# A two-layer transformer kernel: the weights of 16 experts loaded into the queries' place, the first expert's rows alone, and early sums placed behind a normalisation

## What is computed

```
x1  = layernorm(x + attention(x))        # 16 heads of 128+64, latent keys and values of rank 64, causal
top 8 of 64 experts per token (softmax of x1 @ router.T)
moe[t] = sum over its 8 experts e of  w[t,e] * (silu(g) * u) @ down[e],  g, u = split(x1[t] @ gate_up[e])
x2  = layernorm(x1 + moe)                # gate_up: 64 x 256 x 192, down: 64 x 96 x 256
f, i, v, q = x2 @ w_f, ...;  state = tanh(f) * state + sigmoid(i) * silu(v)     # a scan over the tokens
x3  = layernorm(x2 + silu(q * state) @ w_ro + ((x2 @ w_up) * silu(x2 @ w_gate)) @ w_down)
out = layernorm(x3 + shared expert + the top 2 of 8 larger experts)
```

## Time and profile before

| | |
|---|---|
| median of 3 runs | 835.47 us (831.17 to 835.5) |
| the profiled execution's own time | 835.53 us |
| its span in the profile | 833.7 us |
| PE busy | 780.8 us, 94% |
| DVE, ACT, POOL busy | 565.5, 397.6, 272.0 us |
| attention, to its last score block | to 412 us of the span |
| 64 experts | 428 to 537 us |
| mixing | 547 to 621 us |

### The profile page before, as it was taken

How to read it: one execution, slowest core, us unless ns; L and a number is a source line. 1 busy time by engine, 2 the same in 40 slices (tenths; PEclk the granted TensorE clock), 3 DMA queues, 4 the chain that set the end, 5 groups by cost and what they waited for, 6 DMA issues and landing times.

```text
span 833.7 us, 16672 instructions
## 1 busy us (share of the span) xinstructions
PE 780.8 (94%) x4645; PEld 662.9 (80%) x4645; DVE 565.5 (68%) x1422; ACT 397.6 (48%) x898; POOL 272.0 (33%) x357
## 2 busy tenths in 40 slices
PE   7999989999999999999897999998889999999997
PEld 6888867778778777777697898897888778888786
DVE  5323778777877777777644677458857367777766
ACT  1325656655566666666323444312333256666531
POOL 2004445443343333230354565614422500000061
PEclk9998999999999999999998999999998999999999
DMA  7449961000000000000559999777720335555431
GB/s 210 105 104 370 405 238 41 28 28 28 28 21 28 21 18 24 14 28 15 167 157 342 355 357 360 260 254 251 304 102 20 107 112 151 153 151 151 120 94 65
DMA packets 63032, 120.63 MB, mean 145 GB/s; under 512 B 18304, under 2 KB 31616, under 8 KB 62848
## 3 DMA queue, kind: packets, MB, share of 16 engines
q1 hardware_dynamic: 51984, 95.41, 34.9%
q0 software_dynamic: 7680, 21.51, 7.2%
q10 hardware_dynamic: 3312, 3.02, 1.0%
HBM read 76.13 MB, written 43.78 MB: 144 GB/s over the span
## 4 chain that ended last, share of the span: by engine, by line
PE 69%; DVE 12%; issue 7%; ACT 4%; DMA 3%; POOL 3%; SPq 1%; DVEq 0%; ACTq 0%; POOLq 0%
PE scores L1578 9%; PE scores L1577 9%; PE scores L1576 9%; PE probsT_ps L1687 6%; PE scores L1797 5%; PE acc_ps L1987 5%; PE acc_ps L1714 4%; PE misc_ps L1702 4%; PE misc_ps L1700 3%; DVE xT_lo L1054 2%; PE misc_ps L1584 2%; DVE neg_max L1048 2%; PE scores L1807 2%; POOL xd_d L729 2%; PE scores L1840 2%
## 5 line engine op out<-in xcount | busy, mean ns | idle before, releaser
L778 ACT ACTIVATE area<-scores,neg_max 128x128 f32<-128x128 f32 (+7 forms) x128 | 94.9, 742 | 76.7 <-DVE neg_max L1048 75.7
L1048 DVE TENSOR_REDUCE neg_max<-scores 128x1 f32<-128x128 f32 (+7 forms) x128 | 95.7, 749 | 24.6 <-PE scores L1663 24.5
L1687 PE MATMUL probsT_ps<-ident,area 128*128 128x128 f32 x552 | 84.1, 277 | 12.9 <-DVE xT_lo L1054 12.0
L1054 DVE TENSOR_TENSOR xT_lo<-probsT_ps,xT_hi 128x512 fp32r<-128x512 f32 x92 | 62.9, 687 | 38.3 <-ACT xT_hi L785 36.7
L1687 PEld LDWEIGHTS probsT_ps<-ident,area 128*128 128x128 f32 x552 | 63.1, 143 | 24.9 <-issue 19.5
L658 POOL DMA_INDIRECT xe_d<-x_rows,send_i x64 | 64.1, 1001 | 55.8 <-ACT x_rows L802 38.8
L688 POOL DMA_INDIRECT ye_d<-area,home_i x64 | 61.4, 959 | 48.9 <-issue 23.0
L1797 PE MATMUL scores<-area 128*96 128x128 f32 x512 | 68.7, 278 | 1.1 <-DVE area L1220 0.6
L1576 PE MATMUL scores<-kT_hi,weff_hi 128*128 128x512 f32 (+3 forms) x172 | 67.1, 390 | 1.9 <-issue 1.3
L785 ACT ACTIVATE xT_hi<-probsT_ps 128x512 fp32r<-128x512 f32 x92 | 54.0, 594 | 25.1 <-PE probsT_ps L1687 24.8
L1797 PEld LDWEIGHTS scores<-area 128*96 128x96 f32 x512 | 60.5, 166 | 3.2 <-DVE area L1220 2.5
(11 more groups left out here) (258 smaller groups left out, 1944.5 us busy)
## 6 DMA issues: line engine op xcount, KB each, us to landing
area<-gate_up SPq DMA_DIRECT2D x32, 384.0 KB
area<-w SPq DMA_DIRECT2D x23, 512.0 KB, 3.9
xe_d<-area SPq DMA_DIRECT2D x8, 1088.0 KB, 11.3
area<-xe_d SPq DMA_DIRECT2D x32, 272.0 KB, 6.2
ye_d<-area SPq DMA_DIRECT2D x8, 1024.0 KB, 16.7
area<-ye_d SPq DMA_DIRECT2D x16, 512.0 KB, 4.9
area<-w SPq DMA_DIRECT2D x8, 1024.0 KB, 7.3
area<-down SPq DMA_DIRECT2D x32, 192.0 KB
```

The costliest lines, as they stand in the source:

```text
L778: act.activation(row_of(n)[:, 0:L], score_bank(n)[:, 0:L], ACT.Exp, bias=neg_max[:, n % 4:n % 4 + 1], accum_out=rsum[:, s, k:k + 1]).then_ ...
L1048: dve.tensor_reduce(neg_max[:, n % 4:n % 4 + 1], score_bank(n)[:, 0:(n // HEADS + 1) * P], AX.X, ALU.max, negate=True).then_inc(max_ready, 1)
L1054: dve.tensor_tensor(pT_lo[b % 3], seat_of("block", b)[:], pT_hi[b % 3].bitcast(f32), ALU.subtract).then_inc(lo_done, 1)
L1687: last = pe.transpose(seat_of("block", b)[:, i * P:(i + 1) * P], row_of(QUAD * G + i)[:, k * P:(k + 1) * P], ident[:])
```

## The change

The diff does seven things.

- `first_gu`, `first_dn`, `w_c` and `wo_c` are cut from `area1`, where the queries were. After the last split of queries (`q_split`) SP loads the weights of experts 0 to 15 there, in four pairs of transfers of 4 experts, and right behind them `w_c` and `wo_c`. `gate_up` and `down` read experts 0 to 15 from there.
- The ring of weights starts at expert 16. Its first 8 experts are loaded behind the rows of experts 8 to 14, with no wait of their own; from expert 24 on it is as before.
- The rows of expert 0 are loaded alone after send 0 has landed, those of expert 1 alone after send 1. Each has a semaphore.
- The rows of expert 8 and on follow the rows of expert 6 directly.
- The loops over experts on PE, DVE, ACT and POOL are written out as 64 experts. SP keeps a loop for experts 24 to 63.
- POOL's `sum_early(t + 2)` waits for `x2_done`, that is until DVE has normalised tile t+1.
- `w_c` now lies where experts 0 and 1 of `w1` go, so these two are loaded behind the last normalisation of mixing, and experts 2 to 7 during it.

```diff
+IN_ADVANCE = 16
-        w_c = cutC2(6, HC, HID)
-        wo_c = cutC2(2, HC, HID)
+        cutC1 = carve(area1)
+        w_c = cutC1(6, HC, HID)
+        wo_c = cutC1(2, HC, HID)
+        first_gu = cutC1(IN_ADVANCE * HC * 2 * I0).rearrange("p (e c n) -> p e c n", e=IN_ADVANCE, c=HC)
+        first_dn = cutC1(IN_ADVANCE, HID)[0:I0]
...
-        sent_last = moved[1::2]
+        sent_last = moved[0:2] + [moved[k | 1] for k in range(2, TOP0)]
...
-            sp.wait_ge(pT_ps, blocks_to(GROUPS))
-            for e in range(0, RING, 2):
-                load_weights(e, e)
-            sp.wait_ge(x1_done, TILES)
+            sp.wait_ge(q_split, TILES * PAIRS)
+            for e in range(0, IN_ADVANCE, 4):
+                sp.dma_start(first_gu[:, e:e + 4], gate_up0[:, e:e + 4]).then_inc(ld_first, 16)
+                sp.dma_start(first_dn[:, e:e + 4, :], down0[:, e:e + 4, :]).then_inc(ld_first, 16)
+            sp.dma_start(w_c, w_in).then_inc(ld_wc, 16)
+            sp.dma_start(wo_c, w_mix).then_inc(ld_wc, 16)
...
+            sp.wait_ge(pT_ps, blocks_to(GROUPS))
             for u in range(2):
                 sp.wait_ge(sent[u], 16 * (TILES - 1) * TOP0 // 2)
-            for e in range(0, RING, 2):
-                sp.wait_ge(sent_last[e // 2], 32)
+            for e in range(2):
+                sp.wait_ge(sent_last[e], 16)
+                sp.dma_start(xe[:, e:e + 1, :], xe_v[:, e:e + 1]).then_inc((ld_first_row, ld_xe[0])[e], 16)
+            for e in range(2, RING, 2):
+                sp.wait_ge(sent_last[e], 32)
                 load_rows(e, e)
-            sp.dma_start(w_c, w_in).then_inc(ld_wc, 16)
-            sp.dma_start(wo_c, w_mix).then_inc(ld_wc, 16)
-            with sp.Fori(1, E0 // RING) as i:
+            for e in range(RING, IN_ADVANCE + RING, 2):
+                load_rows(e, e % RING)
+                if e < 2 * RING:
+                    load_weights(IN_ADVANCE + e - RING, e % RING)
+            with sp.Fori(1 + IN_ADVANCE // RING, E0 // RING) as i:
...
-                load_w1(t)
+                if t + 2 < E1:
+                    load_w1(t + 2)
             sp.wait_ge(x3_done, TILES)
+            load_w1(0)
+            load_w1(1)
...
                 if before(t, TILES - 2):
+                    pool.wait_ge(x2_done, t + 2)
                     sum_early(t + 2, u)
...
-            for e in range(RING):
-                transpose_rows(e + 2, (e + 2) % RING)
-                gate_up(e + 1, (e + 1) % RING)
-                down(e, e)
-            with pe.Fori(1, E0 // RING - 1) as i:
...
-            for e in range(E0 - RING, E0):
+            for e in range(E0):
                 if e + 2 < E0:
                     transpose_rows(e + 2, (e + 2) % RING)
```

More of the change, by code:

```diff
@@ L309, in home_turn, with weights_of, await_weights @@
         def home_turn(e, u):
-            return turn(e, u) + (32 if u % 2 else 0)
+            return turn(e, u) + (16 if u < 2 else 32 if u % 2 else 0)
+        def weights_of(e):
+            if e < IN_ADVANCE:
+                return first_gu[:, e], first_dn[:, e, :]
+            return gu_w[:, e % RING], dn_w[:, e % RING, :]
+        def await_weights(eng, e):
+            if e < IN_ADVANCE:
+                eng.wait_ge(ld_first, 8 * IN_ADVANCE)
+            else:
+                eng.wait_ge(ld_gu[e % RING // 2], 2 * turn(e - IN_ADVANCE, e % RING))
         def steps_two(eng, body):
@@ L691, in _ @@
             pool.wait_ge(zeroed, 16 * ZEROINGS)
-            for e in range(RING):
[L693 to L696, removed]
+            for e in range(E0):
+                send_home(e, e % RING)
             def sum_early(t, u):
@@ L835, in _ @@
             expert_act(0, 0)
[L836 to L841, removed]
-                    expert_out(RING * i + u, u)
-            for e in range(E0 - RING, E0):
+            for e in range(E0):
                 if e + 1 < E0:
@@ L1228, in find_mine @@
             def find_mine(e, u):
+                if isinstance(e, int) and e == 0:
+                    dve.wait_ge(ld_first_row, 16)
                 dve.wait_ge(ld_xe[u // 2], turn(e, u))
@@ L1260, in _ @@
             gated(0, 0)
-            for e in range(RING):
-                copy_xeT(e + 2, (e + 2) % RING)
-                gated(e + 1, (e + 1) % RING)
-                if e % 2 == 0:
-                    find_mine(e + 2, (e + 2) % RING)
-                else:
-                    find_home(e + 1, (e + 1) % RING)
-            with dve.Fori(1, E0 // RING - 1) as i:
-                for u in range(RING):
-                    copy_xeT(RING * i + u + 2, (u + 2) % RING)
-                    gated(RING * i + u + 1, (u + 1) % RING)
-                    if u % 2 == 0:
-                        find_mine(RING * i + u + 2, (u + 2) % RING)
-                    else:
-                        find_home(RING * i + u + 1, (u + 1) % RING)
-            for e in range(E0 - RING, E0):
+            for e in range(E0):
                 if e + 2 < E0:
@@ L1780, in transpose_rows @@
             def transpose_rows(e, u):
-                pe.wait_ge(ld_xe[u // 2], turn(e, u))
+                if isinstance(e, int) and e == 0:
+                    pe.wait_ge(ld_first_row, 16)
+                else:
+                    pe.wait_ge(ld_xe[u // 2], turn(e, u))
                 if past(e, 2):
@@ L1791, in gate_up @@
                 pe.wait_ge(xeT_done, e + 1)
-                pe.wait_ge(ld_gu[u // 2], 2 * turn(e, u))
+                await_weights(pe, e)
                 if past(e, 2):
@@ L1797, in gate_up @@
                         last = pe.matmul(half[b][0:I0, part * P:(part + 1) * P],
[L1798 removed]
+                                         weights_of(e)[0][:, c, part * I0:(part + 1) * I0], xeT[:, b, c, :],
                                          start=c == 0, stop=c == HC - 1)
@@ L1806, in down @@
                     pe.wait_ge(ye_done, e - 1)
-                pe.matmul(half[2 + b][:, 0:HID], hT[:, b, :], dn_w[:, u, :], start=True, stop=True).then_inc(ye_ps, 1)
+                pe.matmul(half[2 + b][:, 0:HID], hT[:, b, :], weights_of(e)[1], start=True, stop=True).then_inc(ye_ps, 1)
             transpose_rows(0, 0)
```

13 lines of the change are left out of this document (4 added, 9 removed).

## The result

| | before | after |
|---|---|---|
| median of the runs (lowest to highest) | 834.96 us (831.17 to 835.5, 4 runs) | 824.05 us (820.88 to 828.25, 4 runs) |
| the profiled execution: time, span | 835.5, 833.7 us | 823.25, 821.2 us |
| first to last gate and up of the experts | 105.11 us | 97.85 us |
| first combine to last normalisation of mixing | 75.62 us | 72.22 us |

The ratio is 0.9887, with a 95% interval of 0.9845 to 0.993. The forecast was 823.2 us.

What follows compares the result with a forecast made beforehand. PE, busy 94% of the span, bounds the kernel, so gains come where it idles, runs at the lower clock or waits. Experts 8.2 plus mixing 4.1 make 12.3 off 835.5: 823.2 us, range 819.5 to 828.5.

Steps and rivals of the forecast that it cites:

- Part 1: Experts: 6.8 us of stall and lower clock plus 1.4 at the loops' edges come back, 8.2 in all.
- I take the full 8.2: Experts: the whole difference from undisturbed steps was taken as gain, bounds 6.5 and 9.1 us.
- the 1.4: Last 54 experts: 1.4 us lost at the loops' edges come back with written-out lists, unless transfers can't follow.
- Rival B: Later octets: transfers hold them at their old pace, experts gain 6.8, 824.6 us; chance 0.08, alone or with rival A.
- Part 2: First expert's rows loaded alone: no gain, since 40 identity matmuls cover their landing; bounds 0 and 0.
- Part 3: Mixing's early sums: five normalisations no longer run beside POOL's sum; 4.1 us gained, 2.0 if fully blocked.
- with 5 x 0.1: Mixing: a collision with POOL's sum costs a tenth of a microsecond in each of five tiles, leaving 4.1.
- rival A: Mixing: POOL's sum blocks the value product for its whole length, early sums gain only 2.0, 825.3 us; chance 0.13.
- Part 4: Later loads of w1 for experts 0 and 1, behind mixing's last normalisation: no gain, 25 us of cover.
- C: Experts: rows of expert 8 still come late, some 4 of the 6.8 stay, 827.2 us; chance 0.08.
- E: Mixing: POOL's last normalisation, now behind the sum, delays DVE's line 1332, giving back that gain, 827.3 us; chance 0.03.
- D: Experts: written-out lists starve as code comes through full transfer rings, 25 us lost, 848 us; chance 0.05.

Runs made afterwards that it cites:

- e3: The changed kernel with only the 2 MB of w_c and wo_c moved back behind the rows of experts 6 and 7: 829.29 us.
- e4: The changed kernel with experts 16 to 55 as loops of eight again on PE, DVE, ACT and POOL: 823.13 us.
- e1: The changed kernel without POOL's wait for x2_done before the early sum: 828.72 us.
- e5: The changed kernel with the rows of experts 0 and 1 loaded as a pair behind send 1 again: 866.52 us, where the kernel before took 869.08.
- e6: The changed kernel with ten groups of identity matmuls fewer ahead of the experts: 862.73 us, where the kernel before took 869.08.
- e2: The changed kernel with ACT's silu of the value left in PSUM, so DVE's value product has one SBUF input: 824.03 us.
- e13: The changed kernel again, unaltered, on another chip: 863.38 us (12 runs) against 867.31 before, ratio 0.9946.

## Why the prediction was right, and where it was off

The time is 0.85 us over the forecast by the medians and equal to it by the profiled execution (823.25). Both mechanisms are the ones predicted, and both terms were too large: together they gave 10.66 us instead of 12.3. That the profiled execution still met the forecast is luck. The missing 1.64 were made up by 1.84 in stretches where the sum had nothing: 0.88 ahead of the experts, 0.23 between them and mixing, 0.73 behind it.

**Part 1, 8.2 predicted, 7.26 measured.** The sum had 6.8 for the stall and 1.4 for the loops' edges. The three steps of the stall took 11.45 us and now take 4.58: 6.87 gained, and e3 shows the cause, since 5.8 of it return with the 2 MB alone. The 54 steps behind them gained 1.07 (84.77 to 83.70). The six steps ahead of them lost 0.68 (8.89 to 9.57), which "I take the full 8.2" left out: the rows of experts 4 and 5 came 0.54 late. The prediction looked only at experts 8 and 9. (Its 18 us for the transfers ahead were too few: the 2 MB landed at 391.8 and 394.0 instead of 388, at 313 GB/s instead of 362, which cost nothing 35 us ahead of the experts.) This lateness is not in every execution, it is in e4 (0.59) and not in e1 to e3. The weakest term is the 1.4. An edge does cost the 0.32 us that it takes in e4, but the written-out lists lose as much or more at the end: four steps 1.27 us too long in the changed kernel, and over all four written-out runs 83.70 to 84.98 for the 54 steps, where the kernel before has 84.77 and e4 84.03. The 1.07 is one draw from that spread. Rival B put this lag down to the transfers. For them speaks the wait for rows in the changed kernel, at a DMA share of 1.04; against them, that e1 and e3 wait for DVE's copy instead. What makes the end slow stays open.

**Part 2, nothing predicted, nothing measured.** The cover was the 40 groups of identity matmuls: the first transposes stand 8.9 us behind the first send before and after, in e5 with the pair too, and only fewer groups moved them (e6).

**Part 3, 4.1 predicted, 3.40 measured.** The step that was off is "with 5 x 0.1": the product pays 0.40, not 0.1. I had set the two scans of the last tile against rival A's mechanism, and the mechanism won: the product is held up until the sum ends, and e2 shows by what. The price I worked out for it, 0.5 in each tile, was nearly right. What A had wrong is the time: 5 x (0.93 - 0.40) = 2.65, and mixing gained 3.40. Tile by tile the steps fell by 0.27 in the first (8.73 to 8.46) and by 0.56, 0.62, 0.72, 0.62 and 0.62 in the next five. The first I had set at nothing, and it is nothing that can be told from chance: this step took anything from 8.00 (e4) to 9.21 (e13) in runs with the same code of mixing. In the five, 3.1 in all, 0.1 each is not accounted for.

The Trainium skill (SBUF — State Buffer, "Who interferes with whom") states that a DVE instruction with two SBUF inputs and a GpSimd instruction that reads SBUF contend, and that whichever comes first blocks the other for its whole length. The product and e2 agree with it (0.82 with two SBUF inputs, 0.42 with one). The 1.34 of the normalisation, which the prediction counts for it, are no case of two inputs: it has one of 128x256. The scans of the earlier trace rows, at most 0.58 instead of 0.484 inside POOL's normalisation, which has one large input, do not agree. Nor does a row just ahead of them that the prediction passed over, the product of the last tile itself. First before, then e2, where one of its inputs is in PSUM:

```profile
616.14 0.43 DVE L1314 SCALAR_TENSOR_TENSOR area<-area 128x256 f32<-128x256 f32 x1 [0.79 <-ACT area L865]
```

```profile
603.18 1.23 POOL L735 TENSOR_SCALAR x_rows<-y,mv,rstd 128x256 f32<-128x256 f32 x1
603.20 0.42 DVE L1323 SCALAR_TENSOR_TENSOR area<-area,probsT_ps 128x256 f32<-128x256 f32 x1 [0.78 <-ACT probsT_ps L887]
```

It began 0.04 behind POOL's normalisation and was not held up (0.43); POOL's took 1.48, and 1.23 in e2. So inside the one POOL instruction the product pays nothing and inside the other 0.40, and the prediction's row came from the wrong one. That POOL's sum reads two large inputs and its normalisation one may be why; no run shows it.

**Part 4, nothing.** ACT read its first `w1` at 641.25 instead of 654.49, without a wait: it moved with the rest.

**The rivals.** A came true in its mechanism and for three quarters of its price (0.40 of 0.53 in each tile). B's lag shows at the end of the stage alone, and its cause is not shown. C did not happen to expert 8; its like, late rows, did to expert 4, for 0.5 us. E did not happen: behind the sum the tiles stay regular. D did not happen on the first chip, where 57 of the changed kernel's 63 steps are undisturbed. On the others engines start late as D describes, whatever the cause, but in loops too, and the change is no slower than before.

## What to carry to other kernels

Where a stage begins with a wait for a transfer, ask what was issued in front of it: moving these 2 MB 60 us forward cost nothing. Then look at every early load, not only at the one that was late: another was late by 0.5 to 0.6 us in two of five executions. A gain of one microsecond in such a stage needs several traces of each kernel, since the same lists differed by 1.3 us from one execution to the next. When one engine's long operation is moved off another's short one, write down what it now lies over, with the memory of each operand: an operand in PSUM took the collision away. And a row that is to price a collision must have the same instruction on both engines. How much such a repair is worth depends on how late everything else is, so a gain in the start of a stage should be measured on more than one chip.

## What the runs showed of the hardware

- The changed kernel took 824 us on one chip and 863 on another, the kernel before 835, 869 and 867 on three. Mixing is much the same on all (72.2, 72.0 in e5, 73.0 in e13), the experts are not (97.9, 115.3, 112.6): there engines, ScalarE above all, start late on work that is ready, at least in part at fixed places of their lists. The experts are 14.8 of the 39.7 us by which the span of e13 is longer; 6.3 lie ahead of them and 17.8 behind mixing, which no experiment here bears on.
- A product of 128x256 with two SBUF inputs that begins inside POOL's sum of 128x512 ends 0.29 us behind the sum; with one input in PSUM it is not held up at all. Inside POOL's normalisation of 128x256 the product with two SBUF inputs is not held up either (0.43), and POOL takes 1.48 instead of 1.23. A DVE normalisation with one large SBUF input (1.34 instead of 0.41) is held up by the sum as well.
- After 3.88 us of idle time in e3 the clock was 0.80 and then 0.65 on average in the next stretches (1.50 and 4.00 us); after 0.54 us in the changed kernel the next step was undisturbed.
